# Attention and FFN on one core: four of six probability blocks per head pair turned by transfers and VectorE instead of TensorE

## The reference, cut to what matters

```python
x = x + layernorm(attn(layernorm(x)))       # x: 16 sequences x 256 tokens x 256, fp32
x = x + layernorm(ffn(layernorm(x)))
# attn, 16 heads of 128:
q = rope(x @ Wq.T)
k = rope(kp[..., None, :] * kh[..., None]); v = vp[..., None, :] * vh[..., None]
scores = einsum('bnhd,bmhd->bhnm', q, k) / sqrt(128)       # causal mask
p = softmax(scores, axis=-1)
o = einsum('bhnm,bmhd->bnhd', p, v);  return o @ Wout.T
```

## Time and profile before

| what | us |
|---|---|
| median of 3 runs (1042.63 to 1044.16) | 1042.84 |
| profiled execution, span from first to last instruction | 1040.7 |

### The profile page before, as it was taken

One profiled execution on the slowest core, in us unless ns is written; L12 is line 12 of the kernel. 1 busy time (PEld: TensorE's weight loads), 2 busy tenths in 40 slices (PEclk: granted clock), 3 DMA queues, 4 the chain that ended last, 5 costly groups with the idle time before them and its releaser, 6 DMA issues.

```text
span 1040.7 us, 25126 instructions
## 1 busy us (share of the span) xinstructions
PE 1025.2 (99%) x7859; PEld 985.4 (95%) x7859; DVE 822.8 (79%) x2825; ACT 870.2 (84%) x2399; POOL 936.1 (90%) x926
## 2 busy tenths in 40 slices
PE   7999999999999999999999999999999999999997
PEld 6899999999999999999999999999999999999997
DVE  6868798878887888788788888887777656666665
ACT  5978898989898889898989898889888767777774
POOL 4889999999999999999999999999999758888875
PEclk9999999999999999999999999999999999999999
DMA  7561111112112111111121112111131000000001
GB/s 265 184 184 43 42 63 41 43 52 72 44 32 62 62 42 33 61 63 48 36 70 54 43 51 63 43 42 62 33 113 31 2 1 11 22 32 22 21 22 41
DMA packets 35124, 58.56 MB, mean 56 GB/s; under 512 B 3136, under 2 KB 16000, under 8 KB 34688
## 3 DMA queue, kind: packets, MB, share of 16 engines
q1 hardware_dynamic: 34992, 56.96, 16.9%
HBM read 50.92 MB, written 9.18 MB: 58 GB/s over the span
## 4 chain that ended last, share of the span: by engine, by line
POOL 59%; PE 20%; issue 15%; DVE 0%; POOLq 0%; ACT 0%; ACTq 0%; DVEq 0%
POOL arena L598 15%; POOL arena L621 14%; POOL arena L632 13%; POOL arena L608 12%; PE psum L1016 12%; PE psum L1057 6%; POOL arena L580 1%; POOL arena L556 1%; POOL X L589 1%; PE psum L774 1%; PE psum L1029 1%; PE psum L1038 1%; POOL arena L564 0%; POOLq L302 0%; POOL arena L571 0%
## 5 line engine op out<-in xcount | busy, mean ns | idle before, releaser
L632 POOL TENSOR_TENSOR arena<-arena 128x768 f32<-128x768 f32 x128 | 196.4, 1534 | 8.7 <-DVE arena L1580 8.3
L608 POOL TENSOR_TENSOR arena<-arena 128x512 f32<-128x512 f32 x128 | 174.4, 1363 | 10.0
L1593 DVE SCALAR_TENSOR_TENSOR pt_split<-psum,vh_col,pt_split 128x256 fp32r<-128x256 f32 (+1 forms) x512 | 177.0, 407 | 3.6 <-ACT pt_split L1252 3.0
L598 POOL TENSOR_TENSOR arena<-arena,tables 128x512 f32<-128x512 f32 x128 | 166.6, 1302 | 14.0 <-ACT arena L1222 13.2
L621 POOL TENSOR_TENSOR arena<-arena 128x512 f32<-128x512 f32 x127 | 163.1, 1284 | 0.0
L928 PE MATMUL psum<-arena 128*128 128x256 f32 x512 | 154.1, 383 | 3.1 <-POOL arena L608 1.8
L774 PE MATMUL psum<-wo_hi,o_hi 128*128 128x256 f32 x512 | 152.0, 297 | 0.0
L1233 ACT ACTIVATE arena<-arena 128x256 f32<-128x256 f32 x256 | 128.6, 502 | 26.6 <-DVE arena L1570 20.1
L774 PE MATMUL psum<-xt_lo,wq_hi 128*128 128x256 f32 x512 | 144.6, 282 | 0.0
L774 PE MATMUL psum<-xt_hi,wq_lo 128*128 128x256 f32 x512 | 144.4, 282 | 0.0
L774 PE MATMUL psum<-wo_hi,o_lo 128*128 128x256 f32 x512 | 144.2, 282 | 0.0
(11 more groups left out here) (194 smaller groups left out, 3411.7 us busy)
## 6 DMA issues: line engine op xcount, KB each, us to landing
arena<-kh_rows SPq DMA_DIRECT2D x127, 256.0 KB, 3.2
out<-spare SPq DMA_DIRECT2D x15, 256.0 KB, 2.2
arena<-w_rows SPq DMA_DIRECT2D x6, 512.0 KB, 4.7
X<-L_attn_Wout SPq DMA_DIRECT2D x1, 2048.0 KB, 14.3
X<-L_attn_x SPq DMA_DIRECT2D x1, 2048.0 KB, 12.7
arena<-L_attn_Wq SPq DMA_DIRECT2D x1, 1536.0 KB, 9.8
X<-L_attn_x SPq DMA_DIRECT2D x1, 1536.0 KB, 9.7
w_rows<-L_ffn_w_gate_up SPq DMA_DIRECT2D x3, 512.0 KB, 8.1
```

The lines of the kernel that those rows point to most:

```text
L598: nc.gpsimd.tensor_tensor(swap, swap, spread, ALU.mult).then_inc(q_sined, 1)
L608: nc.gpsimd.tensor_tensor(q_rot[p % 2], q_cos[p % 2], q_swap[p % 2], ALU.add).then_inc(q_roped, 1)
L632: nc.gpsimd.tensor_tensor(tb, tb, r.unsqueeze(3).to_broadcast([P, HP, 3, P]), ALU.mult).then_inc(p_ready, 1)
L1593: last = nc.vector.scalar_tensor_tensor(pt_lo[p % 2][:, o], b[:, i], vh[:, t, h:h + 1], pt_hi[p % 2][:, o].bitcast(F32), ALU.mult, ALU.sub ...
```

## The change

Of the three blocks of a head, the early-by-early one is still transposed by TensorE. The two blocks of the late queries are turned in another way. The scores' key columns are ordered by groups of 32 within each key block, so that the maxima write T as four groups b of 32 keys, each holding both heads and both key blocks. When GpSimd has normalised T, SP issues four transfers from SBUF to SBUF (`exchange`): the one of group b takes 512 bytes from each of the 128 partitions, and puts partition 4q + a into partition 32b + q, at place a. One step later VectorE, behind the reciprocal, transposes 32 by 32 squares of this buffer into the two PSUM banks, 256 columns per head (`fill_pt`), with a column step of 4 in the destination; this puts the turned blocks where TensorE wrote them before. The row sums are inverted in two instructions, in the order that T's layout needs. ScalarE's `split_pt` waits for the fills (pt_filled) instead of TensorE's transposes; the maxima of pair g wait in addition for the exchange of pair g - 2. The mask is built in two parts, and the first waits on it move.

```diff
+        blocks = sb("blocks", [P, 4 * P])
+        inverses = sb("inverses", [P, 64])
...
+        T_rows = lambda p, j: T[p % 2][:, 0:4 * P].rearrange("p (b j r) -> p b j r", j=HP, r=P // 2)[:, :, j, :]
+        T_early = lambda p, j: T[p % 2][:, (4 + j) * P:(5 + j) * P]
...
+            def exchange(g0, s):
+
+                at = pair_at(g0, s, LAG["softmax"])
+                if at:
+                    g, p, _ = at
+                    sp.wait_ge(p_ready, g + 1)
+                    at_least(sp, pt_filled, (g - 1) * HP + HP)
+                    for b in range(4):
+                        sp.dma_start(blocks[b * 32:(b + 1) * 32, :].rearrange("q (a e) -> q a e", e=P),
+                                     T[p % 2][:, b * P:(b + 1) * P])\
+                          .then_inc(p_exchanged, 16)
...
                     if not is_first(g0, s) and not is_first(g0, s - 1):
                         spread_kh(g0, s + KH_LEAD)
+                    exchange(g0, s)
...
-                    tb = T[p % 2].rearrange("p j (c m) -> p j c m", m=P)
-                    r = rinv[p % 4].rearrange("p (j c) -> p j c", j=HP)[:, :, 0:3]
+                    tb = heads(T[p % 2], P // 2)
                     pool.wait_ge(p_inv, g + 1)
-                    nc.gpsimd.tensor_tensor(tb, tb, r.unsqueeze(3).to_broadcast([P, HP, 3, P]), ALU.mult).then_inc(p_ready, 1)
+                    nc.gpsimd.tensor_tensor(tb, tb, rinv[p % 4][:, 0:12].unsqueeze(2).to_broadcast([P, 12, P // 2]), ALU.mult)\
+                        .then_inc(p_ready, 1)
...
-                        nc.tensor.matmul(sj[:, 0:2 * P], q[:, j, P:N], kt[:, j, :], start=True, stop=True,
+                        by_blocks = kt[:, j, :].rearrange("p (m b c) -> p b m c", m=NT, b=4)
+                        nc.tensor.matmul(sj[:, 0:2 * P], q[:, j, P:N], by_blocks, start=True, stop=True,
                                          skip_group_check=True)
...
                     for j in range(HP):
-                        b = PT_BANK[j]
                         at_least(pe, pt_lo_done, head_count(g - 1, j))
-                        nc.tensor.transpose(b[:, 0:P], tb[:, j, 2 * P:3 * P], ident[:, :])
-                        nc.tensor.transpose(b[:, P:2 * P], tb[:, j, 0:P], ident[:, :])
-                        nc.tensor.transpose(b[:, 2 * P:3 * P], tb[:, j, P:2 * P], ident[:, :]).then_inc(pt_ready, 1)
+                        nc.tensor.transpose(PT_BANK[j][:, 0:P], T_early(p, j), ident[:, :]).then_inc(pt_ready, 1)
...
-            pe.wait_ge(consts, 3)
+            pe.wait_ge(consts, 2)
...
-                        act.wait_ge(pt_ready, head_count(g, j))
+                        act.wait_ge(pt_filled, head_count(g, j))
...
                     if j == 0:
                         at_least(dve, pt_ready, (g - 2) * HP + HP)
+                        at_least(dve, p_exchanged, (g - 2) * 64 + 64)
                     dve.wait_ge(s_ready, head_count(g, j))
...
                     dve.wait_ge(p_exp, head_count(g, HP - 1))
-                    nc.vector.reciprocal(heads(rinv[p % 4], 2), rsum[p % 4].unsqueeze(2).to_broadcast([P, 2 * HP, 2]))\
-                        .then_inc(p_inv, 1)
+                    sums, made = rsum[p % 4].rearrange("p (j t) -> p t j", t=NT), rinv[p % 4]
+                    nc.vector.reciprocal(made[:, 0:8].rearrange("p (b j) -> p b j", j=HP),
+                                         sums[:, 0, :].unsqueeze(1).to_broadcast([P, 4, HP]))
+                    nc.vector.reciprocal(made[:, 8:12].rearrange("p (j h) -> p j h", j=HP),
+                                         sums[:, 1, :].unsqueeze(2).to_broadcast([P, HP, 2])).then_inc(p_inv, 1)
+
+            def fill_pt(g0, s):
+
+                at = pair_at(g0, s, LAG["turn"])
+                if at:
+                    g, p, _ = at
+                    dve.wait_ge(p_exchanged, g * 64 + 64)
+                    for j in range(HP):
+                        dve.wait_ge(pt_ready, head_count(g, j))
+                        nc.vector.transpose(PT_BANK[j][:, P:3 * P].rearrange("p (m q a) -> p m a q", m=NT, a=4),
+                                            blocks[:, :].rearrange("p (a j m c) -> p j m a c", j=HP, m=NT, c=32)[:, j])\
+                          .then_inc(pt_filled, 1)
...
                     invert_sums(g0, s)
+                    fill_pt(g0, s)
```

More of the change, by code:

```diff
@@ L105, in sandwich_kernel @@
         ident_bf = sb("ident_bf", [P, P], BF16)
-        mask = sb("mask", [P, HP * P])
+        mask = sb("mask", [P, 3 * P])
         ones = sb("ones", [P, 1])
@@ L147, in sandwich_kernel @@
         T_at = used[0]
-        T = [carve(HP, 3 * P) for _ in range(2)]
+        T = [carve(HP * 3 * P) for _ in range(2)]
         k_head = [carve(HP, N) for _ in range(2)]
@@ L209, in sandwich_kernel @@
         rsum = [small[:, 16 + 4 * i:20 + 4 * i] for i in range(4)]
-        rinv = [small[:, 96 + 8 * i:104 + 8 * i] for i in range(4)]
+        rinv = [inverses[:, 16 * i:16 * i + 16] for i in range(4)]
         ln1_stat = small[:, 48:60].rearrange("p (t a) -> p t a", a=6)
@@ L273, in sandwich_kernel @@
         k_scaled = sem("k_scaled")
-        s_ready, s_max, p_exp, p_inv, p_ready = (
-            sem(k) for k in ("s_ready", "s_max", "p_exp", "p_inv", "p_ready"))
+        s_ready, s_max, p_exp, p_inv, p_ready, p_exchanged, pt_filled = (
+            sem(k) for k in ("s_ready", "s_max", "p_exp", "p_inv", "p_ready", "p_exchanged", "pt_filled"))
         pt_ready, pt_hi_done, pt_lo_done, o_ready, o_hi_done, o_lo_done, y_added = (
@@ L544, in _ @@
             masked_fill = pool.to_reg(MASKED)
-            nc.gpsimd.affine_select(out=mask[:, P:2 * P], in_=mask[:, P:2 * P], compare_op=ALU.is_ge, fill=masked_fill, base=0,
-                                    pattern=[[-1, P]], channel_multiplier=1).then_inc(consts, 1)
+            late_mask = mask[:, 0:2 * P].rearrange("p (b m c) -> p b m c", b=4, m=NT)[:, :, 1, :]
+            for m, pattern in ((late_mask, [[-32, 4], [-1, 32]]), (mask[:, 2 * P:3 * P], [[-1, P]])):
+                nc.gpsimd.affine_select(out=m, in_=m, compare_op=ALU.is_ge, fill=masked_fill, base=0, pattern=pattern,
+                                        channel_multiplier=1).then_inc(consts, 1)
             def invert_x(c0):
@@ L937, in turn @@
                     g, p, _ = at
-                    tb = T[p % 2]
                     if isinstance(g0, int) and g == 0:
@@ L1228, in exponent @@
                     g, p, _ = at
-                    tb = T[p % 2]
                     at_least(act, p_inv, g - 3)
                     for j in range(HP):
+                        late, early = T_rows(p, j), T_early(p, j)
                         act.wait_ge(s_max, head_count(g, j))
-                        nc.scalar.activation(tb[:, j, 0:2 * P], tb[:, j, 0:2 * P], ACT.Exp, scale=-1.0,
+                        nc.scalar.activation(late, late, ACT.Exp, scale=-1.0,
                                              bias=nmax[p % 4][:, 2 * j:2 * j + 1], accum_out=rsum[p % 4][:, 2 * j:2 * j + 1])
-                        nc.scalar.activation(tb[:, j, 2 * P:3 * P], tb[:, j, 2 * P:3 * P], ACT.Exp, scale=-1.0,
+                        nc.scalar.activation(early, early, ACT.Exp, scale=-1.0,
                                              bias=nmax[p % 4][:, 2 * j + 1:2 * j + 2],
@@ L1562, in maxima @@
                     g, p, _ = at
-                    tb = T[p % 2]
                     if j == 0:
                         at_least(dve, pt_ready, (g - 2) * HP + HP)
+                        at_least(dve, p_exchanged, (g - 2) * 64 + 64)
                     dve.wait_ge(s_ready, head_count(g, j))
+                    if isinstance(g0, int) and g == 0 and j == 0:
+                        dve.wait_ge(consts, 4)
                     nc.vector.memset(gate_mark[:, j:j + 1], 0.0)
-                    nc.vector.tensor_tensor_reduce(tb[:, j, 0:2 * P], S_BANK[j][:, 0:2 * P], mask[:, :], -1.0, -MASKED,
+                    nc.vector.tensor_tensor_reduce(T_rows(p, j), S_BANK[j][:, 0:2 * P], mask[:, 0:2 * P], -1.0, -MASKED,
                                                    ALU.add, ALU.min, nmax[p % 4][:, 2 * j:2 * j + 1])
-                    nc.vector.tensor_tensor_reduce(tb[:, j, 2 * P:3 * P], S_BANK[j][:, 2 * P:3 * P], mask[:, P:2 * P], -1.0,
+                    nc.vector.tensor_tensor_reduce(T_early(p, j), S_BANK[j][:, 2 * P:3 * P], mask[:, 2 * P:3 * P], -1.0,
                                                    -MASKED, ALU.add, ALU.min, nmax[p % 4][:, 2 * j + 1:2 * j + 2])\
```

## The result

The changed kernel takes 1109.94 us, median of 4 runs (1108.31 to 1112.8), beside 1042.78 us of the kernel before on the same chip: a ratio of 1.0643 [1.0623, 1.0663], 67 us slower. The forecast was 1087 with 1051 to 1135. The direction was right, and so was the ring as the main cause; the size was 23 us short, because the transfers were priced at nothing and cost 26 us. The profiled execution spans 1106.6 us, against 1040.7 before.

A forecast was written before the change was run, and what follows sets the result against it. The VectorE-ScalarE loop bounds the kernel: 0.94 + 3.64 + 1.51 + 0.42 + 0.10 = 6.61 us per step, 0.32 over 6.29, so 41 us plus 3 at the end: 1087 us, range 1051 to 1135.

The forecast's parts named there:

- the ring: VectorE and ScalarE handing work to each other, maxima to next maxima: 5.63 us serial against a 6.29 us mean step.
- Rival B: TensorE sets the pace, fills cost nothing in VectorE's idle time: faster, at most 23 us; 9%.
- The point that I gave for it: TensorE-pace rival decides if the pair of fills adds under 0.38 us to the VectorE-ScalarE loop.
- The fills: Two VectorE transposes of 128x256 between reciprocal and line 1602: 0.35 us each, 0.70 per step.
- The second reciprocal: Added on VectorE ahead of line 1602: 0.12 us per step at most.
- The exposed work: VectorE's other work between reciprocal and line 1602, formerly hidden in the o_hi wait: 0.42 us per step.
- ScalarE's lateness: Extra ScalarE work behind the query swap starts the exponentials late in some steps: 0.1 us per step.
- The exchange: SBUF-to-SBUF transfers issued by SP after line 632's product: at worst 6.6 us from the reciprocal, likely 5.2; costed at nothing.
- The cover of 6.85: Time from a reciprocal to the fill needing its transfer: 6.61 + 0.24 = 6.85 us, one step.
- Rival A: Transfer becomes the new wait, last piece landing 3.9 us after issue: 57 us more, 1144 us; 12%.
- The end of attention: Nothing overlaps the last pair's transfer there: 3 us more.
- rival D: TensorE's clock drops to 1.2 GHz from 0.8 us idle time per step: near 1730 us; 2%.

The follow-up runs named there:

- e5: e1 with the two fills moved ahead of the reciprocal in VectorE's queue, same instructions: 1039.63 us, 0.9973 of the kernel before.
- e1: Changed kernel without the exchange and the waits on it, the fills reading a buffer of zeros: 1084.03 us, 1.0399 of the kernel before.
- e6: Changed kernel with four transposes per pair given back to TensorE as dummies into unused columns: 1108.92 us, 1.0632 of the kernel before.
- e2: e1 without the fills too, leaving TensorE's relief, the second reciprocal and the new layout: 1035.22 us, 0.9929 of the kernel before.
- e7: Changed kernel with GpSimd's product cut in two, the transferred part first, fills still behind the reciprocal: 1098.3 us, 1.0542 of the kernel before.
- e4: Changed kernel, exchange kept, with the two fills moved ahead of the reciprocal: 1151.78 us, 1.1065 of the kernel before.

## Why the prediction was right, and where its numbers came out

**What bounds the kernel: right.** The ring's length, not TensorE's 99%, decided. e5 against e1 shows it by place alone (44 us, same instructions), e6 shows that TensorE no longer matters. Rival B, that the fills fit into idle time and TensorE's relief is a gain, is excluded by e1; its ceiling of 23 us was 7 in e2. The point that I gave for it (the fills add under 0.38 us) was off: they add 0.08 + 0.30 = 0.38 us, and e1 is still 42 us slower than the kernel before. The step without fills is 6.23 (e2), so they had only 0.06 to spare against 6.29.

**The fills: right.** 0.34 each against 0.35 taken, 0.43 long. The successor starts 0.34 after a fill starts, and doesn't wait for its end. The Trainium skill (VectorE: DVE Perf Modes, The DRAIN you can't avoid) says that the next instruction does not start until the pipe is empty, and in the same paragraph that one which is not held starts earlier. The prediction gave the first sentence alone and drew 18 us from it; here two fills took 0.68 and not 0.86, which agrees with the second.

**The second reciprocal: over-sized**, 0.04 instead of 0.12, or 10 us too many. **The exposed work and ScalarE's lateness: under-sized.** The bare step was put at 6.09 and measured 5.95; what comes on top was put at 0.42 + 0.10 = 0.52, and to reach e1's 6.61 it takes 0.66. The two errors of 0.14 cancel, which is why e1 meets the forecast step so exactly. That exactness is luck. No run tells how the 0.66 is made up.

**The exchange: the step that failed.** "I cost it at nothing; its cover is one step, and it is gone where GpSimd is late by over a microsecond." It cost 26 us. Its parts, one by one: from the reciprocal to the end of the product 1.80, as forecast (0.24 + 1.56). Four issues took 2.49 and not 1.6, 0.62 each against the 0.40 that I had read from the spread of kh. The last part landed 4.1 us after the product's end (the median over the steps), so 5.9 after the reciprocal and not 5.2. The cover of 6.85 was too generous as well, since it goes by the mean step: in a bare step the next fill can start 5.95 + 0.2 us behind the reciprocal, so only some 0.3 us are left. Rival A had the right wait and too high a price (57 us): it made every step late, while 21 of them were, and a transfer of the exchange lands 2.2 us behind its issue, not 3.9. The sign that I gave, GpSimd late by over a microsecond, is not what these waits show. In 14 of the 21, with 20.0 of the 24.9 us, the last piece landed over 4.6 us behind the first issue (in 6 of them GpSimd was 0.6 us late as well); in 4, with 1.4 us, GpSimd alone was late, by 0.6 us. What e7 gives back (12 us) is the part that an earlier start cures, and most of the 14 us it doesn't are single late landings.

**The end of attention:** 3 us guessed; the tail behind the last reciprocal grew by 2.1 us. **The clock:** a granted clock of 1.00 in 300 to 400 us, the level of 2.4 GHz, and 0.99 over the profiled execution, where TensorE pauses in every step; rival D didn't occur. **The other signs:** GpSimd 91.0 (92 forecast), a fill's mean 430 ns (420), reciprocals 6.78 apart (6.6). VectorE's share was 89.2, not above 90. The longer steps of the exchange are not the reason, since it is 89.39 in e1; the runs leave it open.

## What to carry to other kernels

Before putting work on an engine with idle time, follow one step around its dependences and ask whether the work stands on that ring: measured from e2, the same two instructions cost 49 us behind the reciprocal (e1) and 4 us under the wait ahead of it (e5). A full engine's relief is worth no more than the distance to the next limit (56 us of TensorE's time gave 7). If a transfer has to land within one step, take the shortest step as its cover, and count its issue time per DMA and its rare late landings. And look twice before its consumer goes ahead of the work that releases the next transfer: here each late landing was then handed on, and e4 came out 42 us slower than the changed kernel.

## What the runs showed of the hardware that was not expected

A transfer of the exchange, 64 KB from SBUF to SBUF in 128 pieces of 512 B, takes 0.60 us to issue on SP (median). The 256 KB spread of kh took 0.32 before (median of line 475; two in a row, with the gap, are the 0.40 each of the earlier trace rows). The source view after (ns min/median/max):

```profile
L489 SPq DMA_DIRECT2D blocks<-arena x512: 547/602/1247, 30.0 to 893.4; - x171
```

So issue time doesn't follow the bytes here. It doesn't go by the transfer alone either: right behind an exchange the spread's own issue takes 0.59, with the same bytes. What sets it wasn't isolated. From the page's part 6 (KB each, median us to landing) and part 3 (packets, MB, share):

```profile
blocks<-arena SPq DMA_DIRECT2D x512, 64.0 KB, 2.2
```

```profile
q8 instruction: 59, 0.97, 0.4%
```

Most of the late landings go together with this instruction queue. Its 59 packets of 16 KB each last 0.88 to 1.59 us, where a piece of 512 B lasts 0.03. Of the 12 exchanges of the changed kernel with the longest time from first issue to last landing, 10 had such a packet under way in between; of the 82 with the shortest, 8 had. The counts of p_exchanged say more: an exchange lands in 64 parts, 16 for each transfer, and in 9 of these 10 just one part came later than 4.5 us. In the step shown above, 63 of the 64 had landed 4.05 us behind the first issue and the last one came at 5.82; the packet had run from 3.17 to 4.68. The two without a packet are of another kind, with all their parts late: once-only loads were under way in the one (1.8 thousand packets of 1 KB, a wait of 4.1 us), and ternary weights in the other (2.2 us). All this is a coincidence in the trace, not a test. The kept trace doesn't name the DMA engine of a packet, and no run here took the instruction packets away, so this cause of the single late landings is likely but open.
